# One transformer layer with test-time training: the same 689 steps written in another order

## What is computed

```python
# x: 4 x 512 x 256; 4 heads of 64; chunks of 128 tokens; carry W0 W1 W2, M0 M1 M2 per head
x = layernorm(x); qkv = x @ Wqkv; q, k, v = silu(qkv) by heads, q and k normalised
for each of the 4 chunks:                      # a scan: the weights carry over
    out = (silu(q @ W0.T) * (q @ W2.T)) @ W1.T
    dw0, dw1, dw2 = gradients from k, v, W0, W1, W2, learning rates
    dw = dw + M * mean(momentum);  M = dw
    X = dw / (|dw| + 1e-7)                     # Newton-Schulz, 5 times:
    for a, b, c in NS_COEFFS:
        A = X @ X.T;  B = b * A + c * (A @ A);  X = a * X + B @ X
    W = renorm(W + X)
attn = windowed softmax attention on the same qkv (window 128)
x = x + layernorm((norm(out) * scale + attn) @ Wo)
x = x + layernorm(gelu(layernorm(x) @ proj1.T + b1) @ proj2.T + b2)
```

## Time and profile before

| | |
|---|---|
| median of 3 runs | 382.53 us (382.41 to 382.57) |
| span of the profiled execution | 380.1 us |
| PE busy | 371.0 us, 98% |
| DVE, ACT, POOL busy | 257.6, 213.3, 193.9 us |
| granted TensorE clock, mean | 0.999 |

### The profile page before, as it was taken

One profiled execution on the slowest core, in us unless ns is written; L12 is line 12 of the kernel. 1 busy time (PEld: TensorE's weight loads), 2 busy tenths in 40 slices (PEclk: granted clock), 3 DMA queues, 4 the chain that ended last, 5 costly groups with the idle time before them and its releaser, 6 DMA issues.

```text
span 380.1 us, 15979 instructions
## 1 busy us (share of the span) xinstructions
PE 371.0 (98%) x6760; PEld 295.4 (78%) x6760; DVE 257.6 (68%) x682; ACT 213.3 (56%) x432; POOL 193.9 (51%) x290
## 2 busy tenths in 40 slices
...
DMA packets 12677, 10.84 MB, mean 29 GB/s; under 512 B 4544, under 2 KB 12096, under 8 KB 12608
## 3 DMA queue, kind: packets, MB, share of 16 engines
...
...
## 4 chain that ended last, share of the span: by engine, by line
PE 86%; DVE 4%; SPq 3%; issue 2%; POOL 2%; ACT 1%; DMA 1%; POOLq 0%; DVEq 0%; ACTq 0%
PE pair L782 15%; PE pair L793 15%; PE pair L713 6%; PE pair L701 6%; PE pair L691 6%; PE pair L559 6%; PE pair L682 5%; PE pair L591 4%; PE pair L763 3%; PE pair L732 3%; PE pair L568 3%; PE pair L748 3%; PE pair L662 2%; PE pair L739 2%; PE pair L629 1%
## 5 line engine op out<-in xcount | busy, mean ns | idle before, releaser
L782 PE MATMUL pair<-xn2T,p1T 128*128 128x512 f32 (+1 forms) x160 | 59.1, 512 | 0.0
L793 PE MATMUL pair<-p2T,h 128*128 128x256 f32 x256 | 57.0, 379 | 0.0
L793 PEld LDWEIGHTS pair<-p2T,h 128*128 128x128 f32 x256 | 48.0, 190 | 6.4 <-issue 0.2
L1424 POOL TENSOR_SCALAR var<-mv 128x1 f32<-128x1 f32 (+1 forms) x55 | 13.1, 239 | 67.1 <-DVE mv L1382 37.4
L1034 ACT ACTIVATE h<-pair,b 128x512 f32<-128x512 f32 (+1 forms) x40 | 23.9, 602 | 36.0 <-PE pair L782 35.9
L782 PEld LDWEIGHTS pair<-xn2T,p1T 128*128 128x128 f32 x160 | 28.7, 190 | 17.1 <-issue 14.8
L1419 POOL TENSOR_TENSOR nq<-ssq,half 128x8 f32<-128x8 f32 (+1 forms) x16 | 24.2, 1513 | 27.5 <-DVE ssq L1141 27.5
L1056 DVE SCALAR_TENSOR_TENSOR A<-pair,eye 128x512 f32<-128x512 f32 x45 | 28.7, 683 | 13.2 <-PE pair L691 13.1
L1419 POOL TENSOR_TENSOR rstd<-var,neg_half 128x1 f32<-128x1 f32 (+1 forms) x55 | 33.5, 609 | 4.6
L1056 DVE SCALAR_TENSOR_TENSOR B<-pair,eye 128x512 f32<-128x512 f32 x45 | 28.9, 684 | 10.2 <-PE pair L701 10.0
L559 PE MATMUL pair<-wqkv,xnT 128*128 128x512 f32 x64 | 31.5, 627 | 0.6 <-ACT xnT L816 0.6
...
## 6 DMA issues: line engine op xcount, KB each, us to landing
...
```

Source lines behind the costliest of these rows:

```text
L782: mm_ = pe.matmul(ps[:, at], p1T[:, k, n * P:(n + 1) * P], xn2T[:, k, at], start=(k == 0), stop=(k == KC - 1))
L793: mm_ = pe.matmul(ps[:, 0:DIM], h[:, n, b * P:(b + 1) * P], p2T[:, n, :], start=(n == 0), stop=(n == HC - 1))
```

## The change

Only the list `ORDER` changes: the same 689 steps, each once, in another sequence. The bodies of the steps, `RISES`, and `bank_plan` are as they were; the banks follow from the list. In the old list the Newton-Schulz steps stand mostly by kind, three weights at a time (TX TX TX, NA NA NA, NB NB NB, NX NX NX); in the new one the three weights are one step apart, so that one weight's NX, the next one's NB and the third one's NA stand side by side, with one TX between such rows. Other steps move too. Two lines of each list, from chunk 2, iterations 0 and 1:

```diff
-    NA.2.0.1 SI.3.0 NA.2.0.2 WO.2.0 WO.2.1 NB.2.0.0 NB.2.0.1 NB.2.0.2 NX.2.0.0 NX.2.0.1 NX.2.0.2 WON.2.0 WON.2.1
-    L2.2.0 TX.2.1.0 TX.2.1.1 TX.2.1.2 PV.2.3 NA.2.1.0 NA.2.1.1 NA.2.1.2 NQ.3.0 F2N.1.2 L2N.2.0 VV.3.1 VV.3.2 NB.2.1.0
+    TX.2.1.0 NR.3.0 NX.2.0.1 NB.2.0.2 NA.2.1.0 CT.2.3 TX.2.1.1 L2.2.1 NX.2.0.2 WON.2.2 NB.2.1.0 NA.2.1.1 NQ.3.1
+    TX.2.1.2 F2N.1.2 L2.2.2 NX.2.1.0 L2N.2.0 NB.2.1.1 NA.2.1.2 SI.3.2 TX.2.2.0 WO.2.3 NX.2.1.1 NB.2.1.2 NA.2.2.0
```

More of the change, by code:

```diff
@@ L136 @@
 ORDER = steps("""
[L137 to L166, removed]
@@ L167 @@
-    F2.1.3 XT.3 GB.2.0 GB.2.1 EL.2.0 EL.2.1 OUT.2.0 OUT.2.1 S.2.1 ELB.2.0 ELB.2.1 OE.2 QK.3.0 QK.3.1 QK.3.2 MU.2.0
-    MU.2.1 MU.2.2 DW.2.0 DW.2.1 PT.2.0 PT.2.1 QK.3.3 MR.2.0 MR.2.1 MR.2.2 SS.2.0 S.2.2 SS.2.1 SS.2.2 S.2.3 OY.2 SN.2.0
-    PV.2.0 PV.2.1 SN.2.1 SN.2.2 PT.2.2 VV.3.0 PT.2.3 PV.2.2 CT.2.0 F2N.1.1 CT.2.1 TX.2.0.0 TX.2.0.1 TX.2.0.2 NA.2.0.0
-    NA.2.0.1 SI.3.0 NA.2.0.2 WO.2.0 WO.2.1 NB.2.0.0 NB.2.0.1 NB.2.0.2 NX.2.0.0 NX.2.0.1 NX.2.0.2 WON.2.0 WON.2.1
-    L2.2.0 TX.2.1.0 TX.2.1.1 TX.2.1.2 PV.2.3 NA.2.1.0 NA.2.1.1 NA.2.1.2 NQ.3.0 F2N.1.2 L2N.2.0 VV.3.1 VV.3.2 NB.2.1.0
@@ L172 @@
[L172 to L181, removed]
@@ L182 @@
-    F2N.2.1 F2N.2.2 F2N.2.3 F1.3.6.0 NT.3.3 F1.3.7.0 L2N.3.3 F1.3.0.1 F1.3.1.1 F1.3.2.1 F1.3.3.1 F1.3.4.1 F1.3.5.1
-    F1.3.6.1 F1.3.7.1 F2.3.0 F2.3.1 F2N.3.0 F2.3.2 F2N.3.1 F2.3.3 F2N.3.2 F2N.3.3
+    LN1.0.0 XT.0.0 LNX.0.0 LN1.0.1 LN1.0.2 CO.0 LN1.0.3 LNX.0.1 QK.0.0 LNX.0.2 VV.0.0 XT.0.1 LNX.0.3 SI.0.0
+    NQ.0.0 XT.0.2 QK.0.1 WI.0 VV.0.1 VV.0.2 NR.0.0 XT.0.3 SI.0.1 QK.0.2 LN1.1 NQ.0.1 SI.0.2 QK.0.3 VV.0.3 NQ.0.2
+    WX.0.0 SI.0.3 TR.0.0 LNX.1 NR.0.1 NQ.0.3 WX.0.1 TR.0.1 TR.0.2 TR.0.3 NR.0.2 SM.0 TR.0.4 TR.0.5 TR.0.6 XT.1
@@ new lines @@
+    WX.0.2 NR.0.3 WN.0 TR.0.7 KL.0.0 MS.0 SP.0 DH.0 VV.1.0 VV.1.1 KL.0.1 GB.0.0 TR.0.8 TR.0.9 VV.1.2 FW.0.0
+    KL.0.2 FW.0.1 GB.0.1 EL.0.0 FE.0.0 FE.0.1 ELB.0.0 EL.0.1 KL.0.3 EY.0 ELB.0.1 QK.1.0 OE.0 OUT.0.0 OUT.0.1
+    QK.1.1 S.0.0 MU.0.0 MU.0.1 S.0.1 MR.0.0 MR.0.1 DW.0.0 DW.0.1 MU.0.2 QK.1.2 S.0.2 SS.0.0 PT.0.0 MR.0.2 OY.0
+    QK.1.3 PT.0.1 SS.0.1 S.0.3 PT.0.2 SN.0.0 SS.0.2 PV.0.0 VV.1.3 PV.0.1 TX.0.0.0 SN.0.1 PV.0.2 PT.0.3 CT.0.0
+    SN.0.2 NA.0.0.0 CT.0.1 TX.0.0.1 WO.0.0 TX.0.0.2 NB.0.0.0 NA.0.0.1 WR.0 SI.1.0 WON.0.0 WO.0.1 NX.0.0.0
```

40 lines of the change are left out of this document (added).

## The result

| | before | after |
|---|---|---|
| median of the runs shown | 382.54 us | 402.53 us (401.78 to 403.35) |
| span of the profiled execution | 380.1 us | 401.3 us |
| ratio | | 1.0524, 95% interval 1.0506 to 1.0542 |

A forecast was written before the change was run, and what follows sets the result against it. PE was taken as the bound, busy 371.0 of 380.1 us. Islands +2.4, hand-overs -1.9 and waits elsewhere -0.9 gave -0.4, so 382.1 us from 382.5; own range 381.0 to 383.2, with rivals 379.7 to 385.6.

The forecast's parts named there:

- PE never stands long: Reading of the old profile: PE's waits for DVE, A and B are short, so its steps' own time sets the length.
- the largest queue place: Chunk 2, iteration 0: NB's last matmuls and NX wait 0.5 us, taken as evictions queueing on DVE.
- Rival B: Evictions queue behind each other in the new Newton-Schulz rows of all three chunks: slower, taken at 384.9 us, chance 0.26.
- Rival C: Third weight's renormalisation comes late at WX.2.2 in chunk 2: 2.8 us more, 384.9 us, chance 0.07.
- Islands +2.4: Seven more runs of small-tile steps between other PE work, 61 instead of 54, cost PE 2.4 us for switching.
- Hand-overs -1.9: Waits for evictions inside the three Newton-Schulz stretches fall by 1.9 us, as the even rows shorten DVE's and ACT's queues.
- Waits elsewhere -0.9: PE's waits outside the Newton-Schulz stretches fall from 2.5 to 1.6 us, two places gone and some new.
- Table loads, nothing: Five more table loads on ACT, 6.4 us of an engine idle 44% of the time, cost nothing.
- The aside on the Trainium skill: Claim that F1's matmul times contradict the page's rule that weight loads overlap matmuls only when row groups differ; no size.

The follow-up runs named there:

- e9: Old list with seven wide steps moved into runs of three small-tile steps, 61 islands instead of 54, against the old kernel: 388.7 us, ratio 1.0172.
- e6: New list with each NA, NB, NX thinned to 8 PE instructions instead of 64, products left out, against the old list thinned likewise: 377.1 us.
- e5: Old list with each NA, NB, NX thinned to 8 PE instructions instead of 64, products left out, as base for the new list thinned likewise: 373.9 us.
- e12: Old list with three islands fewer, by moving MM.1, TR.3.4 with S.3.0 and S.3.1, and DH.1, against the old kernel: 387.3 us, ratio 1.0134.
- e10: Old list with ACT loading its Gelu table again ahead of five F1 steps, 27 loads instead of 22, against the old kernel: 382.3 us, ratio 1.0003.
- e4: Old list's places, with the TX, NA, NB, NX steps filled in the new diagonal order, against the old kernel: 414.1 us, ratio 1.0809.
- e11: New list with NX.1.4.2 and RN.1.2 ahead of F2.1.1, so the third renormalisation starts earlier, against the old kernel: 403.1 us, ratio 1.0536.
- e7: New list with 32 more small matmuls (128 PE instructions) ahead of the first step, against the unchanged new list: 405.9 and 412.5 us.

## Why the prediction was wrong

The step that failed is the first one, "PE never stands long", carried over to the new list, and its inventory of what makes PE's time: own time, islands, and waits for DVE and ACT. The supply of instructions is not in it, and so stood in the sum at nothing, though the earlier trace rows had its mark; the runs showed 15.1 to 17.4 us for it (15.1 with 0.1 us taken off each stop). The row that I called the largest queue place ("NB's last matmuls and NX wait 0.5 us") is a fetch stop: NB stood after 27 of 32 instructions, at number 193, released by "issue" and not by A. No rival had this mechanism, so the range ended at 385.6. B and C had the sign, for other reasons.

- *Islands +2.4*: right as priced. By starts, the own time and islands of the new list are 2.4 longer, and e9's seven made them 2.5 longer.
- *Hand-overs -1.9*: PE's list of waits has none for A or B, but nothing was gained. By starts, and with the stops taken off whole, the three stretches have 4.2 us of waits in the new list and 4.3 in the old one (an estimate: what each step takes beyond the time usual for its kind). Without stops (e6 against e5) the new list's waits are 2.3 us more, not 2.8 less, 2.0 of it at WX.2.2.
- *Waits elsewhere -0.9*: wrong in sign, though small. Up to TX.0.0.0 the waits are 4.0 us, where before had 3.6 with 1.8 of them in QK.0.0, which took 3.55 us to the next start and 1.79 in the new kernel's profile: 2.2 more elsewhere (DH.0 0.7, VV.0.2, QK.0.1, DW.0.0). The granted clock reads 1.00 there in both profiles, so why the first QK is slow in one of them stays open; e9 and e12, which begin like the old list, have it fast too, and then wait up to 1.3 us for `raw` and 0.8 for `rows_b`, so it is not a difference of the lists.
- *Table loads, nothing*: right (e10).
- *Rival B*: not in the changed kernel; e4 shows how it looks. *Rival C*: its place was right, 1.4 us where it had 2.8, its mechanism not: DVE's order, not POOL's power, as the traces of e11 and of the new kernel show it.
- *What was not in the sum*: the stops, 17.4 us whole (17.8 against 0.47) or 15.1 with 0.1 us taken off each, shown by e6 and e7, and by the late packet in e9. With the islands' 2.4 and the 1.4 at WX.2.2 that is the 21.2 us of the span; what else changed is small and cancels.
- *The aside on the Trainium skill*: it gives half of the rule. The same section of "TensorE: Matmul & The Clock Gate" also lets a weight load go ahead of matmuls in flight when it is written to the background weight buffer. F1's eight matmuls in 3.63 us agree with that half, so they don't speak against the page, and no term hangs on it.

What stays open: why the stops stand at number 193 (63 instructions ahead of the first one in the trace would put them at the border of a block, but no run shows those), what fills the 1.2 to 1.6 us between landing and use, and why packets are asked for at such different times (1.2 to 2.5 us behind the last block in the same program at 56 us, in four traces).
